# Splitting weights two pieces a step, and announcing each engine's loop-closing branch, in a fused attention and expert-bias kernel

## The reference

```python
q, k, v = h @ Wq.T, h @ Wk.T, h @ Wv.T      # 32 query heads, 8 key/value heads of 128; rope on q and k
scores  = q_chunk @ k_chunk.T * decay        # chunks of 128 tokens
y       = scores @ x_chunk + (q_chunk * exp(G)) @ state
state   = state * chunk_decay + k_dec.T @ x_chunk
y       = y / rms(y) * gnorm_w * silu(h @ Wg.T)
out     = y @ Wo.T
```

## Time and profile before

| what | value |
|---|---|
| runs | 1928.74 us median of 3 (1928.62 to 1933.93) |
| the profiled execution | 1936.2 us, its span 1934.4 us |
| busy | PE 1735.3 us (90%), DVE 1404.4 (73%), POOL 1225.3 (63%), ACT 1141.4 (59%) |
| granted TensorE clock | mean 0.939 |
| transfers | 77.29 MB, 40 GB/s on average |

### The profile page before, as it was taken

The page is one execution under the profiler, slowest core; times in us unless marked ns, Lnnn a source line. Parts: engine busy times, 40 slices in busy tenths (PEclk is TensorE's granted clock), DMA queues, the critical chain, the costliest instruction groups (busy, mean ns, idle before and its releaser), DMA issues.

```text
span 1934.4 us, 39417 instructions
## 1 busy us (share of the span) xinstructions
PE 1735.3 (90%) x11652; PEld 978.2 (51%) x11652; DVE 1404.4 (73%) x3143; ACT 1141.4 (59%) x3012; POOL 1225.3 (63%) x1153
## 2 busy tenths in 40 slices
PE   5668998989989898989989898989989998999976
PEld 4534454545545454545545454545545454555544
DVE  6976676768867677667767677768867677678875
ACT  5446565656656565656756565656656565656642
POOL 1236676666767576657767676666767576666633
PEclk8779999989999899989999899989999899999997
DMA  4111102010111102010111102010111002100002
GB/s 163 33 34 34 34 18 71 29 41 23 34 61 34 30 17 72 28 41 21 36 57 33 35 17 72 28 41 23 34 61 35 29 17 72 28 29 23 23 1 88
DMA packets 38536, 77.29 MB, mean 40 GB/s; under 512 B 4768, under 2 KB 5792, under 8 KB 37152
## 3 DMA queue, kind: packets, MB, share of 16 engines
q1 hardware_dynamic: 38304, 74.47, 12.3%
HBM read 69.99 MB, written 4.46 MB: 38 GB/s over the span
## 4 chain that ended last, share of the span: by engine, by line
PE 60%; POOL 18%; issue 11%; DVE 4%; ACT 4%; DMA 2%; POOLq 0%; ACTq 0%; DVEq 0%; SPq 0%
PE B L298 18%; PE B L299 18%; PE B L300 18%; POOL QS L1099 4%; POOL WL L1093 3%; PE B L781 2%; POOL WVL L1130 2%; POOL WVF L1122 2%; POOL ROWS L1112 2%; DMA STAGE<-in_wall 2%; POOL RR L1141 2%; POOL QL L1104 1%; ACT XN L417 1%; POOL RM L1138 1%; PE B L447 1%
## 5 line engine op out<-in xcount | busy, mean ns | idle before, releaser
L1134 POOL TENSOR_TENSOR PL<-PF,PH 128x512 bf16<-128x512 f32 x128 | 155.7, 1216 | 390.6 <-ACT PH L934 390.6
L298 PE MATMUL B<-XTH,WH 128*128 128x512 bf16 x640 | 250.5, 391 | 52.8 <-DVE QF L1261 52.1
L934 ACT ACTIVATE PH<-PF 128x512 bf16<-128x512 f32 x128 | 80.5, 629 | 360.2 <-DVE PF L1295 360.2
L298 PE MATMUL B<-WH,XTH 128*128 128x512 bf16 (+1 forms) x1024 | 288.1, 305 | 3.2 <-POOL WL L1093 3.2
L299 PE MATMUL B<-WL,XTH 128*128 128x512 bf16 (+1 forms) x1024 | 286.8, 304 | 0.0
L300 PE MATMUL B<-WH,XTL 128*128 128x512 bf16 (+1 forms) x1024 | 286.3, 304 | 0.0
L299 PE MATMUL B<-XTL,WH 128*128 128x512 bf16 x640 | 250.1, 391 | 0.0
L300 PE MATMUL B<-XTH,WL 128*128 128x512 bf16 x640 | 248.8, 389 | 0.0
L1295 DVE SCALAR_TENSOR_TENSOR PF<-B,DT,PF 128x128 f32<-128x128 f32 x512 | 143.5, 341 | 138.1 <-PE B L300 132.4
L1099 POOL TENSOR_TENSOR QS<-QS,SIN 128x512 f32<-128x512 f32 x160 | 206.1, 1288 | 41.5 <-ACT QS L890 39.9
L298 PE MATMUL B<-WH,ZTH 128*128 128x512 bf16 x512 | 197.4, 386 | 36.5 <-POOL WL L1093 36.5
(11 more groups left out here) (158 smaller groups left out, 4494.6 us busy)
## 6 DMA issues: line engine op xcount, KB each, us to landing
ROWS<-rows_dram SPq DMA_DIRECT2D x128, 256.0 KB, 3.1
STAGE<-in_wall SPq DMA_DIRECT2D x112, 256.0 KB, 2.7
ACC<-in_x SPq DMA_DIRECT2D x4, 1024.0 KB, 7.8
out<-ACC SPq DMA_DIRECT2D x3, 1024.0 KB, 3.9
COS<-in_cos SPq DMA_DIRECT2D x1, 1024.0 KB, 12.8
SIN<-in_sin SPq DMA_DIRECT2D x1, 1024.0 KB, 14.5
out<-ACC SPq DMA_DIRECT2D x4, 256.0 KB, 2.5
EBF<-in_eb SPq DMA_DIRECT2D x1, 256.0 KB, 4.3
```

Source lines behind the costliest of these rows:

```text
L298: nc.tensor.matmul(out_, ah, bh, start=first, stop=False)
L1134: nc.gpsimd.tensor_tensor(PL[:, n % 2, :], PF[:, :], PH[:, n % 2, :], ALU.subtract).then_inc(pl_ready.sem, 1)
```

## The change

The tables now put two pieces in each of seven steps, the even one's low half on POOL and the odd one's on DVE, and the two loads of each pair one working step ahead (pieces 12 and 13 at step 17 in place of 18; 2 to 9 at steps 9 to 12, two each). On ACT the high halves move from behind `decay` to right behind `state_hi`; in step 18 (and 2), where n % 16 is 2, they stand ahead of `square`. On DVE the low halves move behind slots B and C, in step 18 between `zt_lo` and `state_lo`. On POOL they move behind the sine of slot C, in step 18 ahead of `mask_rows`. PE waits for the low halves of pieces 6 to 9 one at a time.

```diff
578.75:601.72 22.97, 22.97 (x139) 11.99 (x138) 15.21 (x32) 14.08 (x40) 15.23 (x15) 1.00 0.09 30 -50,10 +50,10 578.75:601.72 22.97, 22.97 (x139) 11.99 (x138) 15.21 (x32) 14.08 (x40) 15.23 (x15) 1.00 0.09 30
 AFTER_FILL = {0: 3, 1: 2, 3: 2, 5: 2, 7: 3, 8: 2}
 AFTER_FILL_PEELED = {0: 3, 1: 3, 2: 3, 3: 2, 4: 4, 5: 2, 6: 4, 7: 3}
 
-HI = {9: (0,), 10: (1, 2), 11: (3, 4, 5), 12: (6, 7, 8), 13: (9,), 17: (10, 11), 18: (12, 13)}
-LO_POOL = {9: (0,), 10: (1,), 11: (3, 5), 12: (6, 7), 13: (9,), 17: (10,), 18: (12,)}
-LO_DVE = {10: (2,), 11: (4,), 12: (8,), 17: (11,), 18: (13,)}
-LOADS = {3: (0, 1), 9: (2,), 10: (3, 4), 11: (5, 6, 7), 12: (8, 9), 13: (10, 11), 18: (12, 13)}
+HI = {9: (0, 1), 10: (2, 3), 11: (4, 5), 12: (6, 7), 13: (8, 9), 17: (10, 11), 18: (12, 13)}
+LO_POOL = {n: HI[n][:1] for n in HI}
+LO_DVE = {n: HI[n][1:] for n in HI}
+LOADS = {3: (0, 1), 9: (2, 3), 10: (4, 5), 11: (6, 7), 12: (8, 9), 13: (10, 11), 17: (12, 13)}
 POOL_LO = [i for n in sorted(LO_POOL) for i in LO_POOL[n]]
 DVE_LO = [i for n in sorted(LO_DVE) for i in LO_DVE[n]]
 
578.75:601.72 22.97, 22.97 (x139) 11.99 (x138) 15.21 (x32) 14.08 (x40) 15.23 (x15) 1.00 0.09 30 -354,7 +354,7 578.75:601.72 22.97, 22.97 (x139) 11.99 (x138) 15.21 (x32) 14.08 (x40) 15.23 (x15) 1.00 0.09 30
                     load_piece(g + 1 if n >= PEEL else g, i, g)
             for n in range(PEEL):
                 step(0, n, False)
-            with sp.Fori(0, KVH - 1) as g:
+            with nc.Fori(0, KVH - 1, engines=(sp.engine,), hint_back_edge=True) as g:
                 for n in steps(False):
                     step(g, n, False)
             for n in steps(True):
578.75:601.72 22.97, 22.97 (x139) 11.99 (x138) 15.21 (x32) 14.08 (x40) 15.23 (x15) 1.00 0.09 30 -699,8 +699,8 578.75:601.72 22.97, 22.97 (x139) 11.99 (x138) 15.21 (x32) 14.08 (x40) 15.23 (x15) 1.00 0.09 30
                 if fresh:
                     piece = item if item <= PV_ else PG + KT - 1
                     pe.wait_ge(wh_ready.sem, wh_ready.at(gw, piece))
-                    for i in range(PG, PG + KT) if item == PG else (piece,):
-                        signal, k = wl_of(i)
+                    if item <= PV_:
+                        signal, k = wl_of(piece)
                         pe.wait_ge(signal.sem, signal.at(gw, k))
                 if item < PV_:
                     for k in range(KT):
578.75:601.72 22.97, 22.97 (x139) 11.99 (x138) 15.21 (x32) 14.08 (x40) 15.23 (x15) 1.00 0.09 30 -716,6 +716,9 578.75:601.72 22.97, 22.97 (x139) 11.99 (x138) 15.21 (x32) 14.08 (x40) 15.23 (x15) 1.00 0.09 30
                 else:
                     t = t0 + (item - PG) * P
                     for k in range(KT):
+                        if fresh and item == PG:
+                            signal, i = wl_of(PG + k)
+                            pe.wait_ge(signal.sem, signal.at(gw, i))
                         ins = mm3(out_bank[:, :], XTH[:, k, t:t + P], XTL[:, k, t:t + P], WH[:, PG + k, :], WL[:, PG + k, :],
                                   k == 0, k == KT - 1)
                 ins.then_inc(ring_full.sem, 1)
578.75:601.72 22.97, 22.97 (x139) 11.99 (x138) 15.21 (x32) 14.08 (x40) 15.23 (x15) 1.00 0.09 30 -838,7 +841,7 578.75:601.72 22.97, 22.97 (x139) 11.99 (x138) 15.21 (x32) 14.08 (x40) 15.23 (x15) 1.00 0.09 30
 
             for n in range(PEEL):
                 step(0, n, False)
-            with pe.Fori(0, KVH - 1) as g:
+            with nc.Fori(0, KVH - 1, engines=(pe.engine,), hint_back_edge=True) as g:
                 for n in steps(False):
                     step(g, n, False)
             for n in steps(True):
578.75:601.72 22.97, 22.97 (x139) 11.99 (x138) 15.21 (x32) 14.08 (x40) 15.23 (x15) 1.00 0.09 30 -1041,8 +1044,12 578.75:601.72 22.97, 22.97 (x139) 11.99 (x138) 15.21 (x32) 14.08 (x40) 15.23 (x15) 1.00 0.09 30
                     wv_hi(g, n + 1)
                 if n == 0:
                     act.wait_ge(d_sent.sem, 16 * NB)
+                if n % NCH == 2:
+                    next_weights()
                 square(g, n)
                 state_hi(g, n)
+                if n % NCH != 2:
+                    next_weights()
                 if s >= 2 and now:
                     slot("B")
                 if s == 0 and now:
578.75:601.72 22.97, 22.97 (x139) 11.99 (x138) 15.21 (x32) 14.08 (x40) 15.23 (x15) 1.00 0.09 30 -1055,7 +1062,6 578.75:601.72 22.97, 22.97 (x139) 11.99 (x138) 15.21 (x32) 14.08 (x40) 15.23 (x15) 1.00 0.09 30
                 if s == 1 and now:
                     slot("B")
                     hi(g, b + 1, now["A"])
-                next_weights()
                 if s == 1 and now:
                     slot("C")
                 if s == 2 and now:
578.75:601.72 22.97, 22.97 (x139) 11.99 (x138) 15.21 (x32) 14.08 (x40) 15.23 (x15) 1.00 0.09 30 -1063,7 +1069,7 578.75:601.72 22.97, 22.97 (x139) 11.99 (x138) 15.21 (x32) 14.08 (x40) 15.23 (x15) 1.00 0.09 30
 
             for n in range(PEEL):
                 step(0, n, False)
-            with act.Fori(0, KVH - 1) as g:
+            with nc.Fori(0, KVH - 1, engines=(act.engine,), hint_back_edge=True) as g:
                 for n in steps(False):
                     step(g, n, False)
             for n in steps(True):
578.75:601.72 22.97, 22.97 (x139) 11.99 (x138) 15.21 (x32) 14.08 (x40) 15.23 (x15) 1.00 0.09 30 -1173,6 +1179,10 578.75:601.72 22.97, 22.97 (x139) 11.99 (x138) 15.21 (x32) 14.08 (x40) 15.23 (x15) 1.00 0.09 30
 
                 def sine(x):
                     times_sin(g, b + 1, now[x])
+
+                def next_lo():
+                    for i in weights_at(LO_POOL, n, last):
+                        split_lo(g + 1 if n >= PEEL else g, i)
                 if nxt:
                     p_lo(g, n + 1)
                     weighted_v(g, n + 1)
578.75:601.72 22.97, 22.97 (x139) 11.99 (x138) 15.21 (x32) 14.08 (x40) 15.23 (x15) 1.00 0.09 30 -1182,6 +1192,8 578.75:601.72 22.97, 22.97 (x139) 11.99 (x138) 15.21 (x32) 14.08 (x40) 15.23 (x15) 1.00 0.09 30
                     lo(g, b + 1, FILLS[1]["A"])
                 if s < 2 and now:
                     sine("A")
+                if n % NCH == 2:
+                    next_lo()
                 if not (last and n >= NCH - 2):
                     mask_rows(g, n + 2)
                 inv_rms(g, n)
578.75:601.72 22.97, 22.97 (x139) 11.99 (x138) 15.21 (x32) 14.08 (x40) 15.23 (x15) 1.00 0.09 30 -1193,14 +1205,14 578.75:601.72 22.97, 22.97 (x139) 11.99 (x138) 15.21 (x32) 14.08 (x40) 15.23 (x15) 1.00 0.09 30
                     lo(g, b + 1, FILLS[1]["B"])
                 if s == 1 and now:
                     sine("B")
-                for i in weights_at(LO_POOL, n, last):
-                    split_lo(g + 1 if n >= PEEL else g, i)
                 if s == 0 and now:
                     sine("C")
+                if n % NCH != 2:
+                    next_lo()
 
             for n in range(PEEL):
                 step(0, n, False)
-            with pool.Fori(0, KVH - 1) as g:
+            with nc.Fori(0, KVH - 1, engines=(pool.engine,), hint_back_edge=True) as g:
                 for n in steps(False):
                     step(g, n, False)
             for n in steps(True):
578.75:601.72 22.97, 22.97 (x139) 11.99 (x138) 15.21 (x32) 14.08 (x40) 15.23 (x15) 1.00 0.09 30 -1389,6 +1401,10 578.75:601.72 22.97, 22.97 (x139) 11.99 (x138) 15.21 (x32) 14.08 (x40) 15.23 (x15) 1.00 0.09 30
                     else:
                         silu2(g, b + 1, now[x] - PG, use(now[x]))
 
+                def next_lo():
+                    for i in weights_at(LO_DVE, n, last):
+                        w_lo(g + 1 if n >= PEEL else g, i)
+
                 def add(item):
                     add_sin(g, b + 1, item, use(item))
                 if nxt:
578.75:601.72 22.97, 22.97 (x139) 11.99 (x138) 15.21 (x32) 14.08 (x40) 15.23 (x15) 1.00 0.09 30 -1411,6 +1427,8 578.75:601.72 22.97, 22.97 (x139) 11.99 (x138) 15.21 (x32) 14.08 (x40) 15.23 (x15) 1.00 0.09 30
                 update_state(g, n)
                 if n:
                     zt_lo(g, n - 1)
+                if n % NCH == 2:
+                    next_lo()
                 if s < 2 and now:
                     add(now["A"])
                 state_lo(g, n)
578.75:601.72 22.97, 22.97 (x139) 11.99 (x138) 15.21 (x32) 14.08 (x40) 15.23 (x15) 1.00 0.09 30 -1421,17 +1439,17 578.75:601.72 22.97, 22.97 (x139) 11.99 (x138) 15.21 (x32) 14.08 (x40) 15.23 (x15) 1.00 0.09 30
                     add_out(g, n - 2, last)
                 if s == 1 and now:
                     q_lo(g, b + 1, FILLS[0]["C"])
-                for i in weights_at(LO_DVE, n, last):
-                    w_lo(g + 1 if n >= PEEL else g, i)
                 if now:
                     slot("B")
                 if s == 0 and now:
                     add(now["B"])
                     slot("C")
+                if n % NCH != 2:
+                    next_lo()
 
             for n in range(PEEL):
                 step(0, n, False)
```

(2 more changed lines are left out.)

## The result

| kernel | median of runs, us | before, same chip, us | ratio (95% interval) |
|---|---|---|---|
| the change | 1839.37 (1830.42 to 1841.11) | 1930.84 | 0.9516 (0.948 to 0.9551) |
| the change, again, on another occasion | 1835.63 (1832.35 to 1836.55) | 1936.47 | 0.9473 (0.9447 to 0.9499) |

The change saves about 5%, 91 to 101 us, where 141.5 were forecast. 1787 was predicted, with a range that ended at 1828: the sign was right, and both the number and the range were wrong.

A forecast was written before the change was run, and what follows sets the result against it. PE bounds the kernel, losing time to idle waits and lower clock. 149.5 us less 6 (edges) and 2 (step 14) saves 141.5: profiled 1936.2 becomes 1794.7, less 7.5 for the median 1787; range 1774 to 1828.

The forecast's parts named there:

- PE's own work: One loop pass without the stalls, from the lengths of undisturbed steps: 196.8 us, where seven passes took 1520.4.
- the 149.5 us: Time above PE's own work: 142.8 us in seven passes, 0.9 behind the loop, 5.8 in peeled step 2.
- Step 13: With two pieces a step, PE's 7.00 us bank wait and the lower clock go: 7 times about 9.35, or 65 us.
- Step 14: One wait for four low halves (0.4 us) becomes four; residue of 0.3 us each, 2 us in all.
- Step 18: Pieces 12 and 13 load a step earlier; PE's 4.56 us wait at project_out goes, with its share of the clock.
- Next in line is `keys_lo`: Behind the branch, DVE is 1.3 us late against a margin of 0.6; PE waits about 0.7 us at turn_z.
- One of the two stalls comes back in part: Rival: DVE's lateness adds up, step 13's slot A bank is 2 to 3 us late; 35 us, 1822; chance 0.15.
- The branch: PE's six waits at the branch back, 2.7 us each, shrink to 0.3 when announced; with keys_lo's 0.7, 6 us total.
- The announcement brings nothing: Rival: PE's 2.7 us at each branch back stay, DVE pays as much, clock stays low; 28 us, 1815; chance 0.2.
- the 8 us that were booked: Losses taken off the gain: 6 us at the six branches back and 2 us in step 14.
- 1779: Time if the 0.7 us at the edge and all of step 14 go and the clock never falls; low end 1774.
- both smaller losses together: Rival: the announcement fails and one of the two stalls partly returns; 1850 us, chance 0.06.

The follow-up runs named there:

- e6: The change, with both low halves of steps 9 and 17 on POOL, QL earlier, and inv_rms ahead of mask_rows in steps 2 and 18: 1789.91 us, ratio 0.9243.
- e5: The change, with QL (POOL's low half of the fourth query head) right behind the third head's, ahead of mask_rows and inv_rms: 1808.84 us, ratio 0.9339.
- e4: The change, with both low halves of steps 9 and 17 on POOL, so DVE has no split there: 1823.15 us, ratio 0.9415.
- e2: The kernel before, with the announced branches alone: 1908.18 us, ratio 0.9852.
- e1: The change with the plain loops of before, no announced branches: 1833.18 us, ratio 0.9476.
- e7: The change with low halves of steps 9 and 17 on POOL, QL earlier and inv_rms ahead of mask_rows, but plain loops, no announced branches: 1803.3 us, ratio 0.9318.
- e3: The change, with QL (POOL's low half of the fourth query head) one place earlier, ahead of wv_lo: 1811.52 us, ratio 0.9365.

## Why the prediction was right or wrong, point by point

**PE's own work, 196.8 us a pass.** Right to about 1 us: e6 comes to 197.4. The 11.71 us taken for a step 10 hold 0.2 us of a wait that the profile doesn't list (below, step 18); steps 6, 10 and 18 of e6 take 11.50. Nearly all of the 149.5 us above it in the kernel before were there to be won, and most of the miss is that the change does not win them.

**Step 13.** Right in mechanism and size: 13.52 us, as in a step 9, at full clock. Seven times 9.35 us came.

**Step 14.** A residue of 0.3 us was taken; it is 0.44 in each pass, as long a wait as before (0.46 in place of 0.42 in most passes, no clock). But it is another wait: at 545.58, ahead of slot A's seventh product, for POOL's piece 8, which is now split a step later, and not for DVE's piece 9, of which the prediction spoke. So the four separate waits did their part: DVE's low half of piece 9 ends at 546.07, and a wait for all four at slot A's start, about 543.7, would have cost some 2.4 us (an estimate from these times).

**Step 18, the failed step.** The 4.56 us for the low halves went, as worked out. The step that failed is the one that begins "Next in line is `keys_lo`" and ends "which leaves PE about 0.7 us of waiting. That is what is late next." `keys_lo` is not next. The next one is QL on POOL, wanted 3.9 us earlier, by the first product of step 3: PE waited 3.08 us at the branch, where the prediction had 1.0 in all, too short for the clock; and the clock fell behind three of the six. It was to be seen in the trace of before: in the undisturbed step 10 POOL's QL starts at 517.74 and ends at 518.90, and PE's score product starts at 519.13 (the bound of step 11's window):

```profile
517.74 1.16 POOL L1104 TENSOR_TENSOR QL<-QF,QH 128x512 bf16<-128x512 f32 x1
...
518.70 0.38 PE L300 MATMUL B<-WH,ZTL 128*128 128x512 bf16 x1
519.13 0.38 PE L298 MATMUL B<-QH,KH 128*128 128x512 bf16 x1
```

The 0.23 us between QL's end and the product are no margin: in the changed kernel, where PE does wait, the product starts just as far behind QL's end (606.18 to 606.41). The margin was nothing at all. PE's products follow each other every 0.22 us, this one comes 0.43 behind the last, though the profile lists no wait; and where QL comes a microsecond earlier, such a step takes 11.50 us in place of 11.71 (step 10 of e6):

```profile
483.69:495.19 11.50, 11.39 (x76) 6.28 (x75) 9.94 (x23) 8.97 (x24) 10.98 (x12) 1.00 0.24 70
```

By the same measure `keys_lo` had 0.5: its distance is 0.62 us, and 0.13 in e5 and e6, where PE waits for it.

I gave DVE's lateness to the one wait on PE that names DVE, and did not follow the same lateness through ACT's PH into POOL. Against step 10 of before, counted from each step's start, POOL's PL (the low half of the probabilities, made once ACT's PH is there) starts 0.98 us later in step 18 (behind DVE's split of 1.04), POOL's own split puts in 1.30, and `mask_rows` with the first operation of `inv_rms` take 0.80 more (`mask_rows` 1.71 in place of 1.27 us, beside DVE's split and `state_lo`): together 3.08, the whole wait. That DVE's operations are what makes `mask_rows` longer was not tested. e5 and e6 agree with the reasoning on `keys_lo` itself: once QL is away, turn_z waits for it, 1.67 us in e5, of which the edit's own 1.15 leave 0.5, and 0.54 in e6. No run takes QL out of the way and leaves all else as in the change.

**Step 10.** Missed altogether: 1.36 us a pass where 0 was booked. With no margin, all the 1.35 us by which QL ends later in its step reach PE. The rival "One of the two stalls comes back in part" had the cause (DVE's added split in step 9, e4 shows it) but looked for its effect at the bank of step 13, where it isn't. Its counter-argument, that DVE has 2 us idle in each step, was a mean over a step: the idle time lies behind `decayed`, where PE is waited for, and the split comes ahead of it.

**The branch.** The choice near the low end, 0.3 us of 2.7, was right; no cost of an announced branch shows at all (e2, e6). It was also right that the branch of another engine is uncovered once PE arrives early (DVE's 3.1 us, e1). But nothing of it could count here: QL covers it. The rival "The announcement brings nothing" is refuted by e2: six waits for code vanish when the branch is announced. The Trainium skill ("Runtime: NRT & Kernel Launch", Instruction fetch mechanics) calls the prefetch purely sequential; e2 does not agree, and the measurement decides. The pages of the profiles show it from the other side. The queue q8 carries 113 instruction transfers in the three kernels with plain loops (before, e1, e7) and 108 in all seven with announced branches; here before and after:

```profile
q8 instruction: 113, 1.85, 0.4%
```

```profile
q8 instruction: 108, 1.77, 0.4%
```

The time of one such transfer tells nothing of the announcement: in the changed kernel one runs between 602.0 and 603.3 us, ahead of the branch, but so does one in e1, between 601.9 and 603.3.

**The sum.** Of the 52 us between 1787 and 1839, the loop holds 34: seven times 3.05, 1.36 and 0.44 us, together 34, and 7.7 us of clock, behind three of the six waits at the branch and the one at the loop's entry, where I had thought the wait too short for it; less the 8 us that were booked. A further 10 us lie outside the loop: the QL wait at the loop's entry (3.49 us, the same mechanism, in peeled step 2), 1.7 us of clock behind the one at its exit, 1.3 us in the last group (below), and the head and tail, which differ by some us from one profile to the next. The last 8.5 are the basis: the profiled execution of before stood 7.5 us above its median and I carried that over, but the changed kernel's (1838.3) stands 1.0 below its own. The median of before was 1936 to 1939 in the later, larger samples; measured from there the profiled time was ordinary.

**The range.** Its low end is worked out from 1779, which takes off all 8 us for edges and step 14; the 0.7 us at six edges and the 2 us of step 14, as the sentence has it, give 1781. This had no part in the miss. The high end was 1828 because the case "both smaller losses together" (1850) was left outside with 0.06. What happened is of that kind: two smaller losses, in other places.

## What to carry to other kernels

When work is added at the end of an engine's step, follow the delay through every engine that it feeds and list the margin of each wait of the bounding engine, smallest first; here the smallest was nothing, and for step 10 it was on an engine that got no more work in that step or the one before. Take a margin from the distance between the releaser's end and the waiting engine's start, less that distance where the engine did wait (0.23 us for QL, 0.13 for `keys_lo`); a distance of 0.23 us was no margin. An engine's idle time in a step covers an added operation only if it lies between that operation and the next one that somebody waits for. Test parts of a change both alone and taken out: the announced branch is worth some 29 us alone, nothing in this change, and 13 us once the next wait is repaired.

## What the runs showed of the hardware that was not expected

**The same wait costs clock or doesn't.** Behind six waits of 3.06 to 3.12 us at the branch, and with the same products behind them, step 3 took 10.85, 10.85 and 10.86 us three times, and 12.55, 13.80 and 12.21 the other times (the windows above show one of each, at 1.00 and at 0.78). In the second profile of the same kernel it fell four times of six. So a price for the clock taken from one such wait is good to some 2 us either way. A shorter wait was no safer: the clock fell behind five of e3's six waits of 2 us and behind all six of e4's 2.6 us at the branch, 1.7 us each time.

**A stall behind a loop with announced branches.** In all seven profiles of kernels with the announcement, ACT stands for 1.27 to 1.51 us in the middle of `square`, 46 to 48 us behind the end of the loop, with nothing that it waits for; in the three without it, it doesn't. DVE too stands once, 19 to 22 us behind that end, for 0.4 to 1.1 us. ACT's stall cost PE up to 1.4 us, once an execution (nothing in e5). In the changed kernel:

```profile
1668.44 0.28 ACT L960 ACTIVATE YF<-B 128x128 f32<-128x128 f32 x1 [1.29 <-issue]
```

Why there, no run tells; it was not followed up.
